# A four-layer graph network: 34 of the 3,248 edge columns fetched row by row by ACT in place of POOL's indirect gathers

## The reference

```
x = layernorm(x + relational_conv_16(x, W0, src, dst, type16))
x = layernorm(x + cosine_attention(x, beta, src, dst))
x = layernorm(x + gatv2_6_heads(x, W_l, W_r, att, bias, src, dst))
x = layernorm(x + relational_conv_bases(x, W3, coeff, bias, loop, src, dst, type8))
```

## Time and profile before

| | |
|---|---|
| times of three runs | 6174.47, 6192.96, 6193.94 us (median 6192.96) |
| span of the profiled execution | 6172.5 us, 31,606 instructions |
| time of the profiled execution itself | not listed apart from the three runs |
| layer 0 from y0's first gather to DVE's last step | some 1,212 us (192 to 1404) |
| layer 1, edge chunks | some 1,269 us (1546 to 2815) |
| layer 2, edge chunks | some 1,612 us (3135 to 4747) |
| layer 3, edge chunks | some 1,195 us (4892 to 6087) |

### The profile page before, as it was taken

The page is one execution under the profiler, slowest core; times in us unless marked ns, Lnnn a source line. Parts: engine busy times, 40 slices in busy tenths (PEclk is TensorE's granted clock), DMA queues, the critical chain, the costliest instruction groups (busy, mean ns, idle before and its releaser), DMA issues.

```text
span 6172.5 us, 31606 instructions
## 1 busy us (share of the span) xinstructions
PE 1601.1 (26%) x6543; PEld 810.8 (13%) x6543; DVE 2873.7 (47%) x7569; ACT 1131.4 (18%) x3424; POOL 3511.2 (57%) x3636
## 2 busy tenths in 40 slices
PE   5531110000000000003376566656564500000002
PEld 1421110000000000001122222222221400000001
DVE  2344444124345455444255555555556632443435
ACT  1100000000000000001155555555555500000000
POOL 4356666756666666664634544454452576666764
PEclk7765555555555555556688888888887655555555
DMA  4211222221222222221123333333334221222222
GB/s 139 106 53 62 67 64 71 67 81 54 58 64 71 62 69 68 64 71 37 49 106 118 140 138 123 130 139 134 118 140 154 69 67 55 64 79 63 79 63 78
DMA packets 185944, 529.62 MB, mean 86 GB/s; under 512 B 70454, under 2 KB 75170, under 8 KB 169480
## 3 DMA queue, kind: packets, MB, share of 16 engines
q1 hardware_dynamic: 65816, 395.51, 16.9%
q0 software_dynamic: 117696, 129.81, 9.2%
q10 hardware_dynamic: 2224, 2.13, 0.1%
HBM read 185.57 MB, written 341.44 MB: 85 GB/s over the span
## 4 chain that ended last, share of the span: by engine, by line
DVE 39%; another core or an unknown queue 27%; issue 14%; PE 11%; ACT 6%; POOL 3%; DMA 0%; DVEq 0%; ACTq 0%; POOLq 0%
DVE AR L1672 11%; DVE AR L514 5%; DVE ps L779 5%; PE ps L1220 4%; POOL AR L190 2%; ACT AR L1371 2%; PE ps L1236 2%; DVE AR L850 2%; DVE AR L1385 2%; ACT AR L1227 1%; DVE AR L364 1%; DVE AR L1662 1%; PE ps L680 1%; DVE AR L803 1%
## 5 line engine op out<-in xcount | busy, mean ns | idle before, releaser
L190 POOL DMA_INDIRECT AR<-xt,Si x2496 | 2404.4, 963 | 1715.2 <-issue 744.3
L190 POOL DMA_INDIRECT AR<-y,R x752 | 711.3, 946 | 531.1 <-issue 228.7
L1385 DVE SCALAR_TENSOR_TENSOR AR<-AR,gf 128x390 f32<-128x390 f32 x780 | 484.2, 621 | 665.8 <-ACT AR L1371 469.9
L1220 PE MATMUL ps<-AR,WLR 128*128 128x512 f32 x1248 | 690.3, 680 | 152.2 <-ACT AR L1227 113.0
L1672 DVE SCALAR_TENSOR_TENSOR AR<-AR,gf 128x128 f32<-128x128 f32 x831 | 295.0, 355 | 470.8 <-DVE AR L1672 386.9
L1371 ACT ACTIVATE AR<-AR 128x64 f32<-128x64 f32 x1664 | 495.4, 346 | 0.0
L1227 ACT ACTIVATE AR<-ps 128x512 f32<-128x512 f32 x624 | 368.5, 591 | 231.3 <-remote 168.1
L779 DVE SCALAR_TENSOR_TENSOR ps<-ps,gf,AR 128x64 f32<-128x64 f32 x831 | 241.9, 291 | 288.2 <-remote 168.4
L514 DVE SCALAR_TENSOR_TENSOR AR<-AR,gf 128x64 f32<-128x64 f32 x831 | 237.2, 285 | 263.6 <-DVE AR L514 173.3
L190 POOL DMA_INDIRECT AR<-s,endi x196 | 215.7, 1101 | 179.5 <-issue 113.4
L1220 PEld LDWEIGHTS ps<-AR,WLR 128*128 128x128 f32 x1248 | 242.2, 218 | 462.2 <-issue 342.1
(11 more groups left out here) (326 smaller groups left out, 3045.4 us busy)
## 6 DMA issues: line engine op xcount, KB each, us to landing
s<-AR SPq DMA_DIRECT2D x51, 3168.0 KB
AR<-xd SPq DMA_DIRECT2D x104, 512.0 KB
s<-AR SPq DMA_DIRECT2D x51, 1024.0 KB
AR<-xt,Si POOLq DMA_INDIRECT x2496
s<-AR SPq DMA_DIRECT2D x53, 512.0 KB
s<-AR SPq DMA_DIRECT2D x51, 528.0 KB
xd<-AR SPq DMA_DIRECT2D x52, 512.0 KB
y<-AR SPq DMA_DIRECT2D x24, 1024.0 KB
```

Source lines behind the costliest of these rows:

```text
L190: g.indirect_dma_start(out=o, out_offset=None, in_=table, in_offset=bass.IndirectOffsetOnAxis(ap=idx, axis=0)).then_inc(S[sem], 16)
L1220: t.matmul(PS[2 + k % 3][:], WLR[:, ch * P:(ch + 1) * P], XT2[:, u % 6, :], start=True, stop=True).then_inc(S["pm"], 1)
L1385: m = v.scalar_tensor_tensor(out=Sv[:, j, 0:HW], in0=Sv[:, j - 1, 0:HW], scalar=gf[:, c * CH + j:c * CH + j + 1], in1=Sv[:, j, 0:HW], op0= ...
```

## The change

34 columns are taken from POOL and fetched by ACT: always the last column (15) of a chunk. `side_plan` lists the chunks: in layer 0 the chunks 11, 15, ... 47 (10 of them), in layers 1 and 3 the chunks 6, 10, ... 50 (12 each), none in layer 2. In each of those chunks POOL issues 15 gathers, and the count that DVE (in layer 2 PE) waits for is 16 lower (`skipped`).

For one column ACT loads its 128 row numbers from `I0` or `Si` into one partition of the new tile `SIX` (one DMA, semaphore `ix`; two halves by turns), then for each 8 rows one `reg_load` of eight registers, and for each row a DMA of one table row, addressed by the register, into the row's partition of the new tile `SIDE` (4 slots, counted on `hw0` to `hw3`, the former `ys0` to `ys3`). `QUOTA` is how many rows ACT issues for each chunk that it passes: 32. When all 128 rows have landed, ACT copies the column from `SIDE` to its place in the ring, after the same wait for a free slot that POOL has, and counts it on `sc`; DVE waits for `sc` ahead of its steps in these chunks. `LAGS` (3) is the number of chunks between the last rows of a column and the chunk that it belongs to.

The place in ACT's program: in layer 0 a new loop over the chunks 5 to 51 (rows, then the copy for the next chunk); in layer 1 each pass has the copy for the next chunk, this chunk's exps, the rows; in layer 3 a loop of rows and copy for the next chunk, in which the copies of `turn3_a` now stand at chunks 7 to 13.

```diff
 def gathered_before(L, b):
+    late += sum(skipped(l, b, NCH) for l in range(L))
+QUOTA = (32, 32, 0, 32)
+LAGS = (3, 3, 6, 3)
+def side_plan(L):
+    first, cols = FR if L == 0 else 0, []
+    while QUOTA[L]:
+        n = len(cols)
+        c = first + (P * (n + 1) - 1) // QUOTA[L] + LAGS[L]
+        if c > NCH - 2:
+            break
+        cols.append(c)
+    return cols
+SIDES = [side_plan(L) for L in range(4)]
+def skipped(L, b, c):
+    ring = (lambda x: x % N0, lambda x: x % 4, lambda x: 2 * (x % NX) + 1, lambda x: x % 4)[L]
+    return sum(16 for x in SIDES[L] if x <= c and ring(x) == b)
+def row_sem(g):
+    return f"hw{g % 4}", 16 * len(range(g % 4, (NL + 1) // 2, 4)) + 16 * P * (g // 4)
...
+        SIDE = sb("SIDE", [P, 4, 65])
+        SIX = sb("SIX", [1, 2 * P], I32)
...
+        def side_index_y(e, idx, L, n):
+            at = sides_before(L) + n
+            col = SIDES[L][n] * CH + CH - 1
+            load(e, SIX[0:1, at % 2 * P:at % 2 * P + P].rearrange("o (p k) -> o p k", k=1), idx[:, col:col + 1], "ix")
+        def side_rows_y(e, tab, idx, L, i, wide):
+            for r in range(QUOTA[L] * i, min(QUOTA[L] * (i + 1), P * len(SIDES[L])), 8):
+                n, p0 = divmod(r, P)
+                at = sides_before(L) + n
+                if r == 0:
+                    side_index_y(e, idx, L, 0)
+                if p0 == 0:
+                    if at >= 4:
+                        e.wait_ge(S[row_sem(at)[0]], row_sem(at)[1])
+                    e.wait_ge(S["ix"], 16 * (at + 1))
+                    if n + 1 < len(SIDES[L]):
+                        side_index_y(e, idx, L, n + 1)
+                e.reg_load(rowr[e], SIX[0:1, at % 2 * P + p0:at % 2 * P + p0 + 8])
+                for k in range(8):
+                    row = e.snap(rowr[e][k], min_val=0, max_val=tab.shape[0] - 1)
+                    load(e, SIDE[p0 + k:p0 + k + 1, at % 4, 0:wide], tab[bass.ds(row, 1), :], row_sem(at)[0])
+        def side_in_a(e, L, c, dst):
+            at = sides_before(L) + SIDES[L].index(c)
+            e.wait_ge(S[row_sem(at)[0]], row_sem(at + 4)[1])
+            s.copy(dst, SIDE[:, at % 4, 0:dst.shape[1]]).then_inc(S["sc"], 1)
+        def side_done(e, L, c):
+            if c in SIDES[L]:
+                e.wait_ge(S["sc"], sides_before(L) + SIDES[L].index(c) + 1)
+        def linear_side_a(e, c):
+            b = c % N0
+            if c >= N0:
+                e.wait_ge(S[f"s_{b}"], 16 * (c // N0))
+                e.wait_ge(S["lin0"], lin_at(c - N0 + 1, 0))
+            side_in_a(e, 0, c, ring0(c)[:, CH - 1, :])
...
-            for j in range(CH):
+            for j in range(CH - (c in SIDES[0])):
                 gather(buf[:, j, :], tab, idx[:, c * CH + j:c * CH + j + 1],
...
+        def side1_a(e, c):
+            if c >= 4:
+                e.wait_ge(S["p1"], 2 * (c - 3))
+            side_in_a(e, 1, c, G1[:, c % 4, (CH - 1) * 65:CH * 65])
...
+        def basis_side_a(e, c):
+            b = c % NBUF
+            if c >= NBUF:
+                e.wait_ge(S["m3"], 4 * (c - NBUF + 1))
+            side_in_a(e, 3, c, GB[:, b, (CH - 1) * D:CH * D])
...
         @block.scalar
+            rowr[e] = [e.alloc_register(f"rowa{k}") for k in range(8)]
...
+            e.wait_ge(S["i0"], 1)
+            for i in range(4):
+                e.wait_ge(S[f"hw{i}"], row_sem(i)[1])
+            for c in range(FR, NCH):
+                side_rows_y(e, y0, I0, 0, c - FR, D)
+                if c + 1 in SIDES[0]:
+                    linear_side_a(e, c + 1)
...
+            e.wait_ge(S["xdi"], 16)
             for c in range(NCH):
+                if c + 1 in SIDES[1]:
+                    side1_a(e, c + 1)
                 exp1_a(e, c)
+                side_rows_y(e, xt1, Si, 1, c, 65)
...
-            for q in range(NG):
-                turn3_a(e, q)
+            e.wait_ge(S["xt"], T0)
+            for c in range(NCH):
+                side_rows_y(e, xt3, Si, 3, c, D)
+                if c + 1 in SIDES[3]:
+                    basis_side_a(e, c + 1)
+                if 7 <= c < 7 + NG:
+                    turn3_a(e, c - 7)
```

More of the change, by code:

```diff
@@ L71, in stored_before, with sides_before @@
     return sum(16 * len(range(b, NCH, n)) for n in (N0, 3, 2, 3)[0:L] if b < n) + late
+QUOTA = (32, 32, 0, 32)
[13 more added lines that the diff above has]
+    return sum(16 for x in SIDES[L] if x <= c and ring(x) == b)
+def sides_before(L):
+    return sum(len(x) for x in SIDES[0:L])
+def row_sem(g):
+    return f"hw{g % 4}", 16 * len(range(g % 4, (NL + 1) // 2, 4)) + 16 * P * (g // 4)
 def bc(a, shape):
@@ L115, in build @@
         names += [f"g_{i}" for i in range(2 * NX)] + [f"s_{i}" for i in range(N0)] + [f"x_{i}" for i in range(3)]
-        names += [f"ys{i}" for i in range(4)] + [f"nod_{i}" for i in range(2)]
+        names += ["ix", "sc"] + [f"hw{i}" for i in range(4)] + [f"nod_{i}" for i in range(2)]
         S = {n: ctx.enter_context(nc.semaphore("k_" + n)) for n in names}
@@ L694, in y0_store_y @@
             e.wait_ge(S["y0ev"], 2 * k + w)
-            load(e, y0v[:, 2 * k * RT0:(2 * k + w) * RT0], ysb0[:, k % 4, 0:w * RT0], f"ys{k % 4}")
+            load(e, y0v[:, 2 * k * RT0:(2 * k + w) * RT0], ysb0[:, k % 4, 0:w * RT0], f"hw{k % 4}")
         xts = arena(20000, NL, 65)
@@ L756, in g1_chunk @@
                 e.wait_ge(S["p1"], 2 * (c - 3))
-            for j in range(CH):
+            for j in range(CH - (c in SIDES[1])):
                 gather(G1[:, c % 4, j * 65:(j + 1) * 65], xt1, Si[:, c * CH + j:c * CH + j + 1],
                        "late" if c == NCH - 1 and j >= CH // 2 else f"g_{c % 4}")
+        def side1_a(e, c):
+            if c >= 4:
+                e.wait_ge(S["p1"], 2 * (c - 3))
+            side_in_a(e, 1, c, G1[:, c % 4, (CH - 1) * 65:CH * 65])
         def x1_chunk(e, c):
@@ L1168, in g2_chunk, with side2_a @@
                 e.wait_ge(S["ap"], 33 * (c - NX + 1))
-            for j in range(CH):
+            for j in range(CH - (c in SIDES[2])):
                 gather(xsv(c)[:, j, 0:D], xt2, Si[:, c * CH + j:c * CH + j + 1], f"g_{2 * (c % NX) + j // 8}")
+        def side2_a(e, c):
+            if c >= NX:
+                e.wait_ge(S["p2"], p2_end(c - NX))
+            side_in_a(e, 2, c, xsv(c)[:, CH - 1, 0:D])
         def x2_chunk(e, c):
@@ L1198, in pt_t @@
                 k = 2 * (c % NX) + q // 2
-                e.wait_ge(S[f"g_{k}"], gathered_before(2, k) + 8 * CH * (c // NX + 1))
+                e.wait_ge(S[f"g_{k}"], gathered_before(2, k) + 8 * CH * (c // NX + 1) - skipped(2, k, c))
+                if q == 2:
+                    side_done(e, 2, c)
             if q == 0:
@@ L1640, in basis_chunk_g @@
                 e.wait_ge(S["m3"], 4 * (c - NBUF + 1))
-            for j in range(CH):
+            for j in range(CH - (c in SIDES[3])):
                 gather(buf[:, j, :], xt3, Si[:, c * CH + j:c * CH + j + 1],
                        "late" if c == NCH - 1 and j >= CH // 2 else f"g_{b}")
+        def basis_side_a(e, c):
[3 more added lines that the diff above has]
+            side_in_a(e, 3, c, GB[:, b, (CH - 1) * D:CH * D])
         def basis_chunk_v(e, c):
@@ L1792, in build @@
         block = ctx.enter_context(nc.Block())
-        chains = {}
+        rowr = {}
         @block.sync
@@ L1925, in _ @@
                 for i in range(4):
-                    e.wait_ge(S[f"ys{i}"], 16 * len(range(i, (NL + 1) // 2, 4)))
+                    e.wait_ge(S[f"hw{i}"], 16 * len(range(i, (NL + 1) // 2, 4)))
                 resort_g(e, 0)
```

11 lines of the change are left out of this document (7 added, 4 removed).

## The result

The changed kernel took 7,280 us (median of 5) against 6,191: ratio 1.1795, 95% interval 1.1768 to 1.1823. The prediction was 6,172 with a range of 6,130 to 6,400. The profiled executions have spans of 7,319.7 and 6,172.5 us.

What follows compares the result with a forecast made beforehand. The prediction took POOL to wait for DVE in steady state, with DVE crawling during POOL's unbroken gathers. Relief of 24 us less 3 us of added waits gave -21, from 6,193 to 6,172 us, range 6,130 to 6,400.

Steps and rivals of the forecast that it cites:

- I take 0.60, nearer to the low end: ACT's row fetches: 0.60 us a row assumed, from a range of 0.37 to 1.04.
- ACT is covered as long as a row costs less than 0.70 us: Layers 0, 1 and 3: ACT's rows need 77 of 99, 59 of 71.9 and 77 of 90 us at 0.60.
- The rival that came true: Rows over 0.70 us make ACT the bound of layers 1 and 3; 6,263 at 0.75, some 6,450 at 0.80; chance 0.24.
- Relief 24 us: Shorter POOL runs end DVE's stalls earlier: 7.5 us in layer 0, 11.4 in layer 1, 5 in layer 3.
- Slow stretches of DVE follow POOL's runs: Layers 0, 1 and 3: DVE crawls while POOL gathers without a pause; in layer 1 0.35 against 1.45 steps a microsecond.
- 34 waits on DVE at 3 us: DVE's added waits for the side copies: 0 to 24 us possible, 3 us taken.
- Index loads and copies: ACT's index load and copy for each column: 34 x 0.65 = 22 us in all, beside an idle engine.
- turn3 "covered": Layer 3: turn3's copies queue behind 256 rows ending 154 us after 4892.6, before DVE's chunk 8 at some 220 us.
- Rival 2: ACT's rows shorten DVE's fast stretches: 107 us in layer 1, 18 in layer 3, some 6,300 in all; chance 0.14.
- Rival 3: The relief doesn't arrive; a shorter run only makes POOL's wait longer: 6,190 to 6,196 us; chance 0.19.
- That POOL waits for DVE: Layers 0, 1 and 3: in steady state POOL waits for DVE, for 9.8 us in layer 0, 12.1 in layer 1.

Runs made afterwards that it cites:

- skip_only: Changed kernel with the 34 columns left out altogether, neither gathered by POOL nor fetched by ACT; ratio 0.994 to the kernel before.
- half_gathers3: Kernel before with only 8 of 16 columns gathered per chunk of layer 3 from chunk 4 on, DVE's work unchanged; ratio 0.9159.
- pause16_b: Kernel before (also pause16) with POOL waiting after each chunk in layers 0, 1 and 3 until gathers landed; 0.9798 with slow stretches, 1.0448 without.
- rows_unused_c: Changed kernel with POOL gathering all columns and ACT fetching its rows too, nobody using them; ratio 1.1886 to the kernel before, with slow stretches.
- filler_act3_b: Kernel before with 24 long-fulfilled waits of ACT added for each chunk of layer 3; ratio 1.0007 on a chip with slow stretches.

## Why the prediction was wrong

**Step that failed:** "I take 0.60, nearer to the low end", and with it "ACT is covered as long as a row costs less than 0.70 us". The row's own price was right: 0.53 us at full rate, with 0.39 from one row to the next and 0.82 for the eight-register load that eight rows share. What was missing is a second price. The one-row DMAs of the earlier trace rows ran at 197 us, before POOL's long runs; the price for ACT's stretches had to be read from an engine working beside POOL's gathers, as DVE does in the earlier trace rows. I described DVE's slow stretches, let the relief follow from them, and never asked whether ACT's new instructions fall under them too. They do, mostly at 0.7 to 1.4 us an instruction, and a row is three and an eighth: 2.3 to 4.3 us where it was measured. By rows of before that would have been 2.2 to 4.4 us a row for two thirds of the time.

**The rival that came true** is the first, given a chance of 0.24 and priced only up to 0.80 us a row. Its formula at the measured means gives 9 x 33 = 297 us for layer 0 (measured 329), 17 x 20.3 = 345 for layer 1 (253) and 12 x 51 = 610 for layer 3 (505). The agreement says little, since where ACT is the bound its mean price is the layer's own length over its rows; and a mean price has no fixed value here, as the 16-row runs show. The wait that the rival named was the right one, the price in it was not.

**The other steps.**
- Relief 24 us: 24 to 48 measured (skip_only); its split over the layers isn't shown.
- Slow stretches of DVE follow POOL's runs: shown by half_gathers3 for layer 3 and by pause16_b for layers 0 and 3. In layer 1 short pauses didn't help.
- 34 waits on DVE at 3 us: no run isolates them.
- Index loads and copies: 0.49 and 0.245 us, not 0.27 and 0.35, on an engine that had no room for them.
- turn3 "covered": a miss, one chunk 134 us longer in rows_unused_c.
- Rival 2, ACT's rows disturbing DVE: not as forecast, DVE's steps in layer 3 were no slower (412 of 780 slow in rows_unused_c, 480 in filler_act3_b), and layer 1 was bound by the exps. In layer 0 the stands ahead of the histogram grew, with 90 us at 32 rows a chunk and some 32 at 8.
- Rival 3, no relief: refuted by skip_only.
- That POOL waits for DVE is true of chips with slow stretches; on the others POOL is the bound at 20.0 us a chunk.

Open: what a slow stretch is, why some chips have none, and why POOL's pauses end DVE's in layers 0 and 3 but not DVE's in layer 1 and not ACT's. That the recording of the trace has a part in them isn't excluded by any run.

No version here is the fastest on both kinds of chip. Without slow stretches it is the changed one (0.991 and 0.992; pause16 1.045), with them pause16 (0.980; changed 1.18).

## What to carry to other kernels

Price work that goes to an idle engine at the rate of engines that run in the same stretch, not at that of the same instruction elsewhere; and count instructions, registers and moves too, since the busy share doesn't show them. Where an instruction's price depends on how long another engine runs without a pause, a mean price measured in one version doesn't hold in the next. Before tuning on the order of 1%, time the kernel before on more than one chip.

## What the runs showed of the hardware

- On some chips, beside runs of POOL's indirect DMAs, there are stretches in which most instructions of DVE and ACT start 0.70 or 1.40 us after the one before, a fulfilled wait or a register move too: 38 ns became 698 (median).
- Each engine's slow stretches are its own. In the changed kernel, after a long wait of DVE, its steps run at full rate within POOL's run while ACT gets 9 rows out in 27 us:

```profile
6004.94 26.77 ACTq L225 DMA_DIRECT2D SIDE<-xt  x9
...
6012.02 6.16 DVE L1770 SCALAR_TENSOR_TENSOR AR<-AR,gf 128x128 f32<-128x128 f32 x16
```

- The Trainium skill ("Runtime: NRT & Kernel Launch", Instruction fetch mechanics) has some 200 ns for each register loaded from HBM; eight from SBUF took 822 ns here, 103 each.
- The Trainium skill's rule that DVE, with two SBUF inputs or in a 2-port mode, and GpSimd block each other ("SBUF — State Buffer", Summary: rules for kernel authors) doesn't account for the slow stretches: it names these two engines alone, and in filler_act3_b ACT's fulfilled waits, which have no operands, come at the same 1.4 us as DVE's steps.
